# A memset on GpSimd in front of each write that places edge rows into buckets

## The reference, cut to what matters

```python
h = jnp.maximum(_layernorm(x, axis=-1), 0.0)
x = x + _L0_gnn_ref(h, edge_attr_64, src, dst, edge_type_16, ...)
...
x = x + _L1_gnn_ref(h, edge_index)          # two times segment_sum(x[src], dst)
...
x = x + _L2_gnn_ref(h, edge_index, ...)     # four times segment_sum, two dense stages
...
# _L3_gnn_ref
seg = edge_index[0]
sums = jax.ops.segment_sum(edge_attr, seg, num_segments=n)
cnt = jax.ops.segment_sum(jnp.ones(...), seg, num_segments=n)
v_e = sums / jnp.maximum(cnt, 1.0)[:, None]
comb = jnp.concatenate([x, v_e, u[batch]], axis=1)
```

## Time and profile before

| | |
|---|---|
| time, median of 3 runs | 4683.87 us (4682.92 to 4687.05) |
| span of the profiled execution | 6104.5 us |
| instructions in it | 83728 |
| POOL busy | 3187.4 us, 3191 instructions |
| PE busy | 3504.6 us |
| DVE busy | 2563.8 us |
| placing writes, line 711 | 1504, 1539.2 us busy |
| gathers of stage 2, line 686 | 1564, 1545.8 us busy |

### The profile page before, as it was taken

How to read it: one execution, slowest core, us unless ns; L and a number is a source line. 1 busy time by engine, 2 the same in 40 slices (tenths; PEclk the granted TensorE clock), 3 DMA queues, 4 the chain that set the end, 5 groups by cost and what they waited for, 6 DMA issues and landing times.

```text
span 6104.5 us, 83728 instructions
## 1 busy us (share of the span) xinstructions
PE 3504.6 (57%) x18191; PEld 1755.8 (29%) x18192; DVE 2563.8 (42%) x7891; ACT 1503.7 (25%) x3741; POOL 3187.4 (52%) x3191
## 2 busy tenths in 40 slices
PE   5377777777777777776324544345365345455347
PEld 2133333333333333333101222112132112222136
DVE  6266666666666666666330020131120021120368
ACT  3133333323323232322211111111111112111158
POOL 2455555555555555555376555645625635626720
PEclk8588888878888887888656676667666667667679
DMA  5333333333333333333123444334324334324256
GB/s 181 93 77 81 81 78 78 77 80 77 77 77 80 77 77 78 80 77 71 38 93 135 145 146 131 119 112 145 107 79 144 111 132 146 108 79 156 79 200 237
DMA packets 593641, 646.86 MB, mean 106 GB/s; under 512 B 423668, under 2 KB 430418, under 8 KB 587261
## 3 DMA queue, kind: packets, MB, share of 16 engines
q1 hardware_dynamic: 374705, 459.40, 23.2%
q0 software_dynamic: 101760, 110.75, 9.2%
q10 hardware_dynamic: 117068, 75.50, 4.1%
HBM read 451.74 MB, written 190.23 MB: 105 GB/s over the span
## 4 chain that ended last, share of the span: by engine, by line
PE 35%; issue 21%; another core or an unknown queue 21%; DVE 10%; DMA 8%; ACT 2%; POOL 2%; DVEq 1%; SPq 0%; ACTq 0%; POOLq 0%
PE bank L1742 10%; PE bank L1743 7%; PE bank L1823 6%; PE bank L1747 6%; DMA ld_all<-adjacency 3%; DMA rel_table<-ld_all 2%; DMA rel_and_z<-adjacency 1%; DVE hid_T L1305 1%; DMA ld_all<-l_sorted 1%; POOL l_sorted L711 1%; DVE hid_T L1326 1%; DVE hid_T L1584 1%; PE bank L1939 1%; PE bank L1771 1%
## 5 line engine op out<-in xcount | busy, mean ns | idle before, releaser
L711 POOL DMA_INDIRECT l_sorted<-arena,l_pos x1504 | 1539.2, 1023 | 1339.3 <-ACT arena L854 877.4
L686 POOL DMA_INDIRECT ld_all<-rel_table,rel_and_z x1564 | 1545.8, 988 | 1133.0 <-remote 503.2
L1742 PE MATMUL bank<-hid_T 128*128 128x400 f16 x2346 | 965.7, 412 | 672.6 <-issue 539.8
L1743 PE MATMUL bank<-hid_T 128*128 128x384 f16 x2346 | 940.5, 401 | 44.3 <-issue 43.5
L1326 DVE TENSOR_SCALAR hid_T<-count_key,hid_T 128x400 f16<-128x400 int16 x2346 | 592.1, 322 | 754.5 <-remote 526.7
L1823 PE MATMUL bank<-rel_and_z,ld_all 128*128 128x512 fp8e4 (+1 forms) x1872 | 522.3, 414 | 602.9 <-issue 534.1
L1823 PE MATMUL bank<-ld_all 128*128 128x512 fp8e4 (+1 forms) x1950 | 511.4, 420 | 337.4 <-issue 138.4
L1747 PE MATMUL bank<-ld_all,arena 128*32 x4692 | 527.1, 250 | 123.3 <-issue 121.3
L1742 PEld LDWEIGHTS bank<-hid_T 128*128 x2346 | 255.9, 109 | 1157.3 <-issue 1153.9
L774 ACT CAST ld_all<-bank 128x400 fp8e4<-128x400 f32 x391 | 191.1, 489 | 1551.6 <-remote 999.7
L1266 DVE COPY accT<-bank 128x512 f32<-128x512 f32 (+1 forms) x78 | 51.1, 656 | 1215.4 <-remote 797.1
(11 more groups left out here) (289 smaller groups left out, 4103.0 us busy)
## 6 DMA issues: line engine op xcount, KB each, us to landing
ld_all<-adjacency SPq DMA_DIRECT2D x72, 1600.0 KB
rel_and_z<-adjacency SPq DMA_DIRECT2D x72, 1600.0 KB
l_sorted<-zeros SPq DMA_DIRECT2D x147, 424.0 KB
arena<-in_edge_attr SPq DMA_DIRECT2D x195, 256.0 KB
ld_all<-l_sorted SPq DMA_DIRECT2D x33, 1277.5 KB, 6.0
adjacency<-ld_all ACTq DMA_DIRECT2D x391, 100.0 KB
rel_table<-ld_all SPq DMA_DIRECT2D x49, 520.0 KB, 3.6
ld_all<-rel_table,rel_and_z POOLq DMA_INDIRECT x1564
```

Source lines behind the costliest of these rows:

```text
L686: pool.indirect_dma_start(ring[:, c % RING, 0:TW], None, rel_table, bass.IndirectOffsetOnAxis(ap=rel_i[:, c:c + 1], axis=0)).then_inc(s(f" ...
L711: pool.indirect_dma_start(l3_sorted, bass.IndirectOffsetOnAxis(ap=l3_pos[0:parts, n * SB_K + k:n * SB_K + k + 1], axis=0), rows16[q][0:par ...
L1742: pe.matmul(b0[:, 0:w0], low[:, 0:P], pair_hot[q % 2][:, k, 0:w0], start=k == 0, stop=k == CG - 1)
L1743: pe.matmul(b1[:, 0:GW - w0], low[:, P:2 * P], pair_hot[q % 2][:, k, 0:GW - w0], start=k == 0, stop=k == CG - 1)
```

## The change

In the loop over the 47 blocks, in front of each of the 32 placing writes, GpSimd fills the first 195 columns of `minus_base` with zeros, 128 x 195 f32. Each of these memsets signals a new semaphore, `paused`, and each but the first waits until the memset before it has signalled. The indirect DMA itself does not wait for the memset by a semaphore; it stands behind it on the same engine.

```diff
@@ -708,6 +708,9 @@
                         pool.wait_ge(s(f"l3_moved{m}"), 16 * SB_K)
                     pool.sem_inc(s("turn"), 1)
                     for k in range(SB_K):
+                        if m or k:
+                            pool.wait_ge(s("paused"), m * SB_K + k)
+                        pool.memset(minus_base[:, 0:NG // 2], 0.0).then_inc(s("paused"), 1)
                         pool.indirect_dma_start(l3_sorted, bass.IndirectOffsetOnAxis(ap=l3_pos[0:parts, n * SB_K + k:n * SB_K + k + 1], axis=0),
                                                 rows16[q][0:parts, k, :], None).then_inc(s(f"l3_moved{q}"), 16)
```

## The result

The changed kernel takes 4867.49 us (median of 4 runs, 4865.59 to 4871.68), the kernel before beside it 4683.4 us (4680.37 to 4687.05). The ratio is 1.0395, 95% interval 1.038 to 1.041: 184 us slower. I had forecast slower, 5125 us, by GpSimd being the bound of stage 3. The direction and the bound were right and the time lies inside the range, but the price of a memset was wrong and the step of 441 us was 2.4 times too large.

The account below looks back on a forecast made before the run. GpSimd was taken to bound stages 2 and 3: 1504 memsets at 0.32 us make 481 us, less 40 hidden, so 4684 + 441 = 5125 us. The 8-in-10 range was 4820 to 5450 us.

Parts of the forecast that it names:

- the step of 441 us: Whole kernel: 481 us of added GpSimd time less 40 us hidden, added to 4684 us.
- GpSimd bounds stage 3 in timed runs: Stage 3: a block holds GpSimd 40.8 us, while the aggregations would ask for one every 21.7 us.
- a floor of 4509 us: GpSimd's time in a timed run, everything else hidden: 203 + 1951 + 176 + 1916 + 263 us.
- The price of a memset, 0.32 us: Before each placing write: memset 0.26 plus 0.06 us, 1504 times, 481 us on GpSimd.
- the low bound: Between placing writes: the memset fills the 0.30 us gap, adding 0.08 us a write.
- the middle value: Between placing writes: the 0.30 us stays and the memset adds its own pitch, 0.32 us; chance 0.58.
- What is hidden, 40 us: Two dense stages: two queued blocks reach 20 us further into GpSimd's idle time in each.
- Moved waits, cost nothing: Block start on GpSimd: split and landing waits move to the first memset; `paused` waits are always met; 0 us.
- Rival 1: Stage 3: ACT, PE and loads set the pace, GpSimd's slack hides the memsets, 4684 us; chance 0.06.
- Rival 2: Stage 3: breaks before writes let PE through, ACT splits earlier, 4378 us at best; chance 0.05.
- Rival 3's low price: Stage 3, GpSimd bound: 0.08 us a write, 120 less 10 us of cover, 4794 us; chance 0.16.
- about 6500 us: Profiled span of the changed kernel: most of the 441 us expected on top of 6104.5 us.

Follow-up runs that it names:

- e1: The kernel before, unchanged, profiled a second time; 4680.24 us in a single run, profiled span 4678.5 us.
- e4: The kernel before without the last 4 of the 32 placing writes of each block, no memsets, sums wrong; 4460.79 us, ratio 0.9526.
- e2: The changed kernel with each memset over 391 columns in place of 195; 5097.74 us, ratio 1.0884 to the kernel before.
- e5: The changed kernel with a block's 32 memsets all in front of its 32 writes; 5097.85 us, ratio 1.0894 to the kernel before.
- e6: The kernel before plus 391-column memsets ahead of the writes of blocks 23, 24, 38 and 39 alone; 4690.05 us, ratio 1.0022.
- e7: The kernel before plus 391-column memsets ahead of the writes of blocks 12, 13, 30 and 31 alone; 4718.47 us, ratio 1.008.
- e11: The kernel before, no memsets, with 17 large DVE TENSOR_TENSOR statements each cut into eight; 4823.65 us, ratio 1.0298.
- e10: The kernel before, no memsets, with 17 large DVE TENSOR_TENSOR statements each cut into four; 4627.52 us, ratio 0.9878.

## Why the prediction was right and wrong

**GpSimd bounds stage 3 in timed runs: right.** This was argued from the pitch of 1.274 us and from a floor of 4509 us, against the waits of the profile. e1 shows ACT waiting 560.7 us for GpSimd, e4 and e2 show the slope on both sides. That the sum came so near was partly luck, since its errors offset each other. I put 211 us of idle time in the dense stages beside the 4509, which are 29.1 us. Left out were the 140 us by which the writes exceed their median, 19 of them in the last block and the rest beside DVE's operations; stage 2 takes 2031 us, not 1951; and between the stages are 98 to 100 us, not the 176 of the disturbed profile. With 80 more in stage 2, 171 more in stage 3 and 76 less between, 4509 gives 4684.

**The price of a memset, 0.32 us: wrong, and the step that failed.** The forecast said "the 0.30 us belongs to the write and the memset adds its own pitch". The runs show that a memset starts in the gap and fills it, as the low bound said, though with 0.17 us and not 0.06 us before the next write. In terms of the sum: memset 0.278 + 0.166 us after it, less 0.305 us, is 0.139 us; with writes 0.009 us longer 0.148 us, near the 0.146 by which the pitch grew from 1.274 to 1.42. By the totals of both profiles, without the idle time ahead of the stage's first instruction, it is 418.6 + 252.2 - 460.5 + 5.6 = 216 us, where 481 stood. The length of the memset was good, 260 ns forecast for 278 measured (261 the shortest). e5 shows that 0.317 us is the price of such a memset behind another one that it waits for. My reason for the middle value was a row of memset behind memset, which is a row about another neighbour.

The rule of the Trainium skill that was weighed beside it (Perfetto Trace Analysis, DMA Instruction — SWDGE (GPSIMD), that the shown end of a write comes before GpSimd is done with it) would have kept part of the gap closed. The timeline shows the memset starting at the shown end, with no idle time. So as far as these rows tell, the trace does not bear out that consequence; the low bound's 0.08 us was missed for the 0.17 us ahead of the next write instead.

**What is hidden, 40 us: right in kind, too large.** GpSimd's waits for ACT fell from 29.1 to 4.8 us, 24 us, and 216 - 24 = 192 us is the step (191.4 between the spans). The reason given, the blocks queued at the start of a dense stage, is what e6 and e7 show. There were three of them, not two, so some 3 x 32 x 0.144 = 14 us before each dense stage: all of the first idle time of 12.0 us, and 12.3 of the 17.1 of the second. The 106.1 and 104.6 us of the earlier trace rows, into which I had let the blocks reach, were those of the disturbed profile.

**Moved waits, cost nothing: right.** The waits for `paused` show no idle time in the timeline, where a write stands between two memsets.

**The rivals.** Rival 1 (hidden, 4684) falls by the 184 us themselves, by e4 and by e2. Rival 2 (faster through PE) had its only support in the disturbed execution: e1 has 384.8 us of waits on PE's weight loads of L1823 in place of the 1264.0 of the earlier trace rows, and GpSimd's waits for ACT are 29.1 us, so there were no 787.5 us to win. Rival 3's low price, 4794 us, was nearer than the forecast; the measured 4867 lies between.

**The profiled execution of the changed kernel**, for which I wrote about 6500 us, has 4869.9. I had expected the difference of 1420.6 us in this profile too. It was one execution's: every profile taken later has the span of its timed runs.

## What to carry to other kernels

Where an engine leaves a regular gap between two instructions of one kind, ask what may start inside that gap before pricing an added one: the same memset cost 0.14 us behind an indirect write and 0.317 us behind another memset, and a short one cost nothing. Compare the profiled span with the timed runs first; when they are 30% apart, profile again before taking its waits as evidence. Here all waits turned round, while the pitch of 1.274 us was the same in both. And slack of the bound engine covers only what is added shortly before it, since lateness further back is passed on round the ring of buffers.

## What the runs showed of the hardware

- Between two indirect writes of GpSimd 0.30 us pass whatever is in it, up to a filling of about 0.14 us: memsets of 1 column (0.12 us) and two of them (0.14 us together) were free, 65 columns (0.172 us) cost 34 us in 1504, 195 columns 184 us, 391 columns (0.442 us) 416 us.
- A large f32 TENSOR_TENSOR of DVE with its inputs in SBUF stretched a GpSimd write that met it, from 0.97 to as much as 5.27 us; a TENSOR_SCALAR of 1.89 us did too (2.59 us), a TENSOR_REDUCE of 3.62 or 5.38 us did not. With the TENSOR_TENSORs cut into four the 1504 writes took 60.6 us less and the kernel 58 us less.
- A change in stage 3 of DVE's program made GpSimd wait 225 us more in stage 2 (e11, 729.9 us before its gathers for 505.1), with 252 packets of instruction fetches for 18. Cut into four, the same statements had not done it (e10). What sets where this begins stays open.
- What held up the first profiled execution of before stays open too; it did not come back in e1.
